# Differential attention and gated recurrence: five score blocks moved between two attention units

## The reference

```python
x = x + attn(layernorm(x))
x = x + ffn(layernorm(x))

# attn: 16 heads of width 16 for q and k, 8 heads of width 32 for v
q, k = rope(x @ Wq.T) * scaling, rope(x @ Wk.T)
probs = softmax(q @ k.T)                       # per head, 1024 x 1024
diff = probs[:, :, 0] - lam * probs[:, :, 1]   # pairs of heads
attn = diff @ v
attn = attn * rsqrt(mean(attn * attn) + 1e-5) * (1 - LAMBDA_INIT)
return attn @ Wo.T

# ffn: a recurrence over the 16 rows of the batch, its state is one 1024 x 256 array here
c = sigmoid(x @ wf.T + c @ uf.T + bf) * c + sigmoid(...) * tanh(...)
h = tanh(x @ wo.T + c_final @ uo.T + bo)
```

## Time and profile before

| | |
|---|---|
| device time, median of three runs | 5032.77 us |
| device time of the profiled execution | 5053.02 us |
| span of the profiled execution | 5051.2 us |
| mean granted clock of TensorE in it | 0.986 |
| busy share of PE, DVE, ACT, POOL | 97%, 78%, 57%, 58% |

### The profile page before, as it was taken

How to read it: one execution, slowest core, us unless ns; L and a number is a source line. 1 busy time by engine, 2 the same in 40 slices (tenths; PEclk the granted TensorE clock), 3 DMA queues, 4 the chain that set the end, 5 groups by cost and what they waited for, 6 DMA issues and landing times.

```text
span 5051.2 us, 67243 instructions
## 1 busy us (share of the span) xinstructions
PE 4895.6 (97%) x24784; PEld 1745.4 (35%) x24784; DVE 3960.6 (78%) x6295; ACT 2884.9 (57%) x5221; POOL 2930.4 (58%) x2134
## 2 busy tenths in 40 slices
PE   7999999999999999999999999999999999999999
PEld 2224242332424233242332424233242433324237
DVE  7888878888887878878887887888788787887526
ACT  1565646656465665646566464665646566564642
POOL 3583837657374674728567383764738477472740
PEclk7899999999999999999999999999999999999999
DMA  6121222303122130222313123230312313022117
GB/s 151 30 56 52 47 66 53 66 32 66 47 47 72 34 76 38 55 59 47 72 34 62 46 47 70 48 66 30 67 48 47 72 34 76 39 47 55 68 51 291
DMA packets 127867, 311.19 MB, mean 62 GB/s; under 512 B 27313, under 2 KB 30514, under 8 KB 113714
## 3 DMA queue, kind: packets, MB, share of 16 engines
q1 hardware_dynamic: 124562, 289.72, 24.1%
q10 hardware_dynamic: 2976, 17.17, 0.9%
HBM read 172.07 MB, written 99.61 MB: 54 GB/s over the span
## 4 chain that ended last, share of the span: by engine, by line
PE 77%; POOL 11%; ACT 5%; DVE 3%; issue 3%; DMA 0%; SPq 0%; ACTq 0%; DVEq 0%; POOLq 0%
PE s_ps L795 15%; PE o_ps L835 15%; PE st L822 14%; PE st L928 13%; POOL pair_sum L484 11%; PE sum_ps L850 7%; PE st L763 4%; PE st L781 4%; ACT probs L591 3%; DVE neg_max L1127 2%; PE st L1005 2%; PE st L906 1%; PE o_ps L750 1%; DVE xa L1114 1%; PE s_ps L1005 1%
## 5 line engine op out<-in xcount | busy, mean ns | idle before, releaser
L484 POOL TENSOR_TENSOR pair_sum<-probs 128x512 f32<-128x512 f32 x2048 | 2822.1, 1414 | 1211.3 <-ACT probs L591 1210.6
L1127 DVE TENSOR_REDUCE neg_max<-s_ps 128x1 f32<-128x512 f32 x4096 | 2582.1, 682 | 700.2 <-PE s_ps L795 697.8
L591 ACT ACTIVATE probs<-st 128x512 f32<-128x512 f32 x4096 | 2162.3, 603 | 971.6 <-PE st L822 810.6
L795 PE MATMUL s_ps<-k_stack,q_stack 96*128 96x512 bf16 x4096 | 1523.0, 389 | 43.5 <-DVE neg_max L1127 37.0
L822 PE MATMUL st<-q_stack,k_stack 99*128 99x512 bf16 x4096 | 1475.8, 385 | 28.7 <-ACT probs L591 7.5
L835 PE MATMUL o_ps<-probs,values 128*32 128x512 f32 x8192 | 1095.3, 607 | 12.2 <-ACT probs L591 8.5
L822 PEld LDWEIGHTS st<-q_stack,k_stack 99*128 99x128 bf16 x4096 | 368.3, 97 | 1360.1 <-ACT probs L591 905.2
L795 PEld LDWEIGHTS s_ps<-k_stack,q_stack 96*128 96x128 bf16 x4096 | 400.7, 98 | 686.0 <-DVE neg_max L1127 336.6
L850 PE MATMUL sum_ps<-pair_sum,ones 128*32 128x512 f32 x4096 | 534.9, 594 | 26.6 <-POOL pair_sum L484 26.6
L928 PE MATMUL st<-pair_sum,weights 128*128 128x512 f32 x768 | 381.9, 594 | 11.8 <-ACT pair_sum L547 11.8
L541 ACT ACTIVATE probs<-st,gate_bias 128x512 f32<-128x512 f32 x192 | 131.7, 686 | 441.7 <-PE st L928 441.7
(11 more groups left out here) (151 smaller groups left out, 2926.6 us busy)
## 6 DMA issues: line engine op xcount, KB each, us to landing
q_stack<-qk_parts SPq DMA_DIRECT2D x384, 128.0 KB, 4.3
k_stack<-qk_parts SPq DMA_DIRECT2D x381, 128.0 KB, 7.0
swapped<-xa SPq DMA_DIRECT2D x128, 256.0 KB, 2.4
qk_parts<-swapped SPq DMA_DIRECT2D x64, 512.0 KB, 2.8
qk_parts<-low_part SPq DMA_DIRECT2D x64, 256.0 KB, 3.0
probs<-in_x SPq DMA_DIRECT2D x16, 1024.0 KB, 9.7
x_rows<-probs SPq DMA_DIRECT2D x16, 1024.0 KB, 3.9
xa<-in_x SPq DMA_DIRECT2D x15, 1024.0 KB, 6.0
```

Of the source, the lines that this page charges most:

```text
L484: pool.tensor_tensor(pair_sum[q % 2][:, h, :], probs[a % 4][:, h, :], probs[(a + 1) % 4][:, h, :], ALU.add)\
L591: act.activation(probs[kk % 4][:, h, :], st[n % BANKS][:, :], ACT.Exp).then_inc(exp_done, 1)
L795: pe.matmul(s_ps[i % BANKS][:, :], q_stack[g][0:SROWS, s, t * P:(t + 1) * P], k_stack[g][0:SROWS, s, h * HALF:(h + 1) * HALF], start=True, ...
L1127: dve.tensor_reduce(neg_max2[:, at, i % 2:i % 2 + 1], s_ps[i % BANKS][:, :], AX.X, ALU.max, negate=True).then_inc(max_done, 1)
```

## The change

The first five score blocks of unit u + 2 leave the attention of the odd unit and go between the units. On PE the order becomes: `turn_max(u + 1)`; the q part of the projection with one score block after its third and one after its fourth matmul; `key_sums(u, 0, 15)`; the k part of the projection, with one score block after its last matmul; two more score blocks; the wait for ACT's four copies; the attention. On DVE two maxima follow `split_shift`, and three follow `finish_sums(u, 0, 3)`. `PLAN1` now spreads blocks 5 to 95 (91 instead of 96), and `WORK` no longer holds anything extra for its steps 0 and 1. In the last row of the batch only the position of the key sums is as it was, and nothing is added.

```diff
+MIDDLE = (2, 3)
@@
-WORK[1][0] += 2
-WORK[1][1] += 3
@@
-PLAN1 = score_plan(0, SCORES - sum(LATE), 1)
+PLAN1 = score_plan(sum(MIDDLE), SCORES - sum(LATE), 1)
@@ PE
-            def qk(g, b, ab, blocks=iter(()), each=(1,) * 8):
-
-                for X in range(2):
+            def qk(g, b, ab, blocks=iter(()), each=(1,) * 8, parts=(0, 1)):
+
+                for X in parts:
@@ PE
                 attention(u, 0, u + 1, PLAN0)
                 turn_max(u + 1)
+                middle = ((u + 2, 0, i) for i in range(sum(MIDDLE)))
                 if not last:
-                    qk(1, b, ab)
+                    qk(1, b, ab, middle, (0, 0, 1, 1, 0, 0, 0, 0), (0,))
                 key_sums(u, 0, 15)
                 if not last:
+                    qk(1, b, ab, middle, (0, 0, 0, 0, 0, 0, 0, 1), (1,))
+                    for block in middle:
+                        score(*block)
                     pe.wait_ge(act_out, ab + QK1 + 4)
                 attention(u + 1, 1, u + 2, NO_PLAN if last else PLAN1)
@@ DVE
                 split_shift(u + 1)
+                if not last:
+                    for i in range(MIDDLE[0]):
+                        maximum(u + 2, i)
                 finish_sums(u, 0, 3)
+                if not last:
+                    for i in range(MIDDLE[0], sum(MIDDLE)):
+                        maximum(u + 2, i)
                 attention(u + 1, 1, u + 2, NO_PLAN if last else PLAN1,
                           None if last else u + 3)
```

## The result

| | before | after |
|---|---|---|
| device time, median of 22 runs each, side by side | 5032.93 us | 5039.0 us |
| ratio after to before, 95% interval | | 1.0012 (1.0007 to 1.0018) |
| span of the profiled execution | 5051.2 us | 5037.6 us |
| one row of the batch, undisturbed | 298.28 us | 298.63 us |

A forecast was written before the change was run, and what follows sets the result against it. PE was taken as the bound, with stretches bounded by POOL. Terms 0.56 - 0.31 + 0.66 - 0.92 + 0.19 gave +0.18 us a passage, times 15 +2.7 us on 5032.8: 5035.5 us, range 5020 to 5051.

The forecast's parts named there:

- first key tile: Start of the odd attention on PE: at about 9.37 us after the turn of the maxima instead of 8.12.
- waiting up to the first value products: PE's waiting from the turn of the maxima, with later blocks paced by DVE's maxima: 1.22 for 0.66 us, +0.56.
- steps 1 to 4: Odd attention, four blocks a step: DVE catches up and score waits of 0.08 and 0.23 go, -0.31 us.
- three blocks fewer beside POOL: Steps 5 to 13, 11 blocks for 14: stretch stays 27.65 us, the freed PE work becomes waiting, +0.66 us.
- after the stretch: Behind POOL's 16 adds: vanished score waits save 0.92 us, a new wait late in the attention costs about 0.19.
- the four pairs of waits: PE's score waits after steps of five blocks, behind POOL's stretch, 0.23 us each: they vanish, -0.92 us.
- step 27: Late step without score blocks: one block instead of two behind the preceding key tile, about +0.19 us of waiting.
- Rival 1: DVE doesn't catch up, four early attention steps each keep 0.23 us of waits: +0.92 us a passage, 5049 us; chance 0.24.
- Rival 2: One blocked add fewer in POOL's stretch, as DVE reaches its rope earlier: -0.99 us a passage, 5021 us; chance 0.14.
- one for one over the whole span: Argument on POOL's adds: 308 long adds for 310 DVE rope instructions, each lengthening one add by about 0.99 us.
- Rival 3: DVE's idle time counts: five maxima done in the gap shorten each passage by 3.0 us, 4988 us; chance 0.04.
- Rival 4: Block 0 between the units holds up the projection for shift or stack: 1 us or more, 15 us slower; chance 0.02.

The follow-up runs named there:

- runs with short adds: Kernel before and changed kernel, each with POOL's pair adds of odd units over half the columns: 5018.5 and 5018.1 us, both against 5033.8.
- plan-only run: Kernel before without the plan's extra work in steps 0 and 1, nothing laid between the units: 5091.8 us against 5033.8.
- hand-written plan: Changed kernel with PLAN1, 3 score blocks in steps 0 and 1, 16 in steps 5 to 13: 5015.2 us against 5033.5.
- run with the key sums alone: Kernel before with only the last key sums moved between the projection's q and k parts: 5047.1 us against 5033.5.
- spread plan: Changed kernel, odd unit's rope instructions spread over steps 5 to 24, 19 score blocks in steps 5 to 13: 4999.8 us against 5033.1.
- fill: Changed kernel with 14 instead of 11 score blocks in steps 5 to 13, three fewer after them: 5029.3 us against 5033.5.

## Why the prediction was right

It held in its sign, its size class and, but for one point, its mechanism: 5039.0 in a range of 5020 to 5051. The size did not come out: a loss of 6.1 us, 0.12%, where 2.7 us, 0.05%, was forecast. Term by term, per passage, with 0.22 us for each score block that lies elsewhere:

| step of the prediction | forecast | measured | from |
|---|---|---|---|
| first key tile | 9.37 us | 9.52 us | stretches |
| waiting up to the first value products | +0.56 | +0.69 | 13.74 - 11.07 - 9 x 0.22 |
| steps 1 to 4 | -0.31 | -0.33 | 12.08 - 12.41 |
| three blocks fewer beside POOL | +0.66 | +0.64 | 27.63 - 27.65 + 0.66 |
| after the stretch | -0.73 | -0.64 | 57.42 - 59.38 + 6 x 0.22 |
| sum | +0.18 | +0.36 | end 110.87 - 110.52 = 0.35 |

- The sum of 0.18 is what is left of terms of up to five times its size, so its sign hangs on errors of 0.1 us. That the misses left the sign as it was is in part luck; two of them, 0.13 and 0.09, point to slower, and they are why 2.7 us became about 5.3.
- The start-up. The k part of the projection gave 0.1 us away behind the key sums: its first record lasts 0.53 us, from 572.98 on, for 0.43 elsewhere. So block 2 starts at 8.67 and maximum 2 at 9.09, where 8.97 was forecast; each later block hangs on that maximum, and this is the 0.13. The forecast let maximum 2 wait for the end of DVE's sums; in the trace it waits for block 2 on PE (0.46 us). The first key tile was sized 0.15 us too early, for the most part by the same 0.1 us (ACT's last copy comes at 8.87 and not at 8.73), but the value products do not hang on it.
- After the stretch the four pairs of waits are gone and step 27 waits 0.19, both as forecast. A key tile of step 16 waits 0.10, which I had not foreseen, and that is the miss of 0.09. A wait of 0.20 more in step 19 is made up for by one of 0.23 less in step 20.
- The three blocks fewer beside POOL. The +0.64 is as forecast, but by the runs with short adds POOL's bound is the reason for about a third of it only (0.64 less 0.44); I had put all of it down to POOL.
- Rival 1, DVE not catching up, did not occur: from the second step on the blocks go at PE's pace. The plan-only run is no case of it either: what cost more there than rival 1's price is one stop of 2.83 us and the lower clock after it.
- Rival 2, a long add fewer, did not occur in the change (27.63 us, eight long adds). The hand-written plan reached it. Against it the prediction set "one for one over the whole span", from 1.265 us for a short add. The trace's short adds are 1.274 us on average, and counted one by one the long adds are 291 for 310 rope instructions. In the odd attentions, which are what counts here, it is ten for ten in all 15 passages.
- Rival 3, DVE's idle time as the currency, fell by the run with the key sums alone.
- Rival 4 fell by the trace: block 0 starts at 2.75 us after the turn (forecast 2.74), without a wait.
- The shared port. A long add for each rope instruction in the stretch, by about 1 us, is what the runs show at eight, seven and five. That agrees with the rule of the Trainium skill, "SBUF — State Buffer", section "Who interferes with whom", that a DVE instruction with two SBUF inputs contends with a GpSimd instruction that reads SBUF and that the port pair is an exclusive lock. The holds go beyond its sentence that the order of issue decides: in the trace of before the four adds after the one that was running started up to 3.8 us after the rope instruction and still went ahead of it. Why DVE loses there and not elsewhere stays open.

So the answer to what the change does: it fills DVE's gap, where nothing was waiting for DVE, at the price of a start-up paced by DVE, and it frees room in a stretch whose length PE does not set. Its gain, the vanished score waits (about -1.0 us a passage), is real and was outweighed. With the plan corrected for these two points the moved blocks do take part in a faster kernel; how much of that kernel's gain needs them was not tried, since no run had the spread plan without them.

## What to carry to other kernels

Give work to a resource's gap only if somebody waits for that resource later; first find, stretch by stretch, which queue sets the length, and put movable work into the stretches that another engine bounds, where it is free (in the run that filled the stretch three blocks there saved 0.66 us behind it, and three put into steps that already waited cost 0.12). When work goes to the front of a phase, look at the pace of the engine behind it in exactly those steps. When a step is moved on one queue, price it on every queue that it touches. And before a slow run is put down to the chip, look in its trace for the one instruction that took several times its usual length.

## What the runs showed of the hardware

- In the plan-only kernel PE stopped for 2.83 us from start to start (3.18 in one passage), with the granted clock at 1.00 before. In each of the 15 passages a stretch at the lower clock followed, 0.52 over 6.67 us in the row shown. The loss was 3.2 to 4.5 us a row of the batch, where 2.0 was expected without the clock. No rule follows from it: in the trace of before, three stops of 3.20 us were followed by the lower clock and a fourth was not.
- A DVE instruction with two SBUF inputs beside POOL's train of adds lengthens one add, from 1.27 to 2.25 us on average, and takes 1.3 to 2.4 us itself; where no add is lengthened, it mostly takes 1.22.
- In 29 of the 4340 rope instructions of the fourteen traces it is the other way round: DVE is held for 4.8 or 6.2 us beside four or more adds, none of them lengthened by more than 0.3 us, and PE then stops for 2.5 to 3.2 us. 22 of the 29 are in the two traces from one chip, 11 of these at one instruction that had been moved.
- Lengths of stretches repeat to a few hundredths of a us over the rows of the batch and from kernel to kernel (27.61 to 27.66 in 15 passages each of before, after and fill), so that terms of 0.1 us in 5000 can be read from one trace where whole times scatter by some us.
